# Second experts of a fused transformer block: the links of a tile's chain two tiles apart, banks by matrix, gates on ScalarE

## The reference

```python
scores = softmax(xf @ Wg.T)
expert_weights, expert_indices = top_k(scores, 2)        # of 8 experts
expert_weights = expert_weights / expert_weights.sum(-1, keepdims=True)
h1 = lora_in(xf, W1, b1, A1, B1)                         # 128 -> 256, per expert
h3 = lora_in(xf, W3, b3, A3, B3)
g = silu(h1) * h3
y_e = lora_out(g, W2, b2, A2, B2)                        # 256 -> 128
y = einsum('te,ted->td', gates, y_e)
```

## Time and profile before

| what | value |
|---|---|
| median of three timed runs | 960.75 us (959.2 to 961.38) |
| profiled execution, from its first to its last instruction | 1025.8 us |
| its time outside this span | not given by the trace |
| TensorE, VectorE, GpSimd, ScalarE busy in it | 741.2, 685.5, 575.1, 456.1 us |
| second experts, first turn to last scatter | 851.33 to 995.89 us |
| transfers in it, mean rate 900 to 960 us | 188 GB/s |

### The profile page before, as it was taken

How to read it: one execution, slowest core, us unless ns; L and a number is a source line. 1 busy time by engine, 2 the same in 40 slices (tenths; PEclk the granted TensorE clock), 3 DMA queues, 4 the chain that set the end, 5 groups by cost and what they waited for, 6 DMA issues and landing times. The chain is left out here.

```text
span 1025.8 us, 21613 instructions
## 1 busy us (share of the span) xinstructions
PE 741.2 (72%) x6690; PEld 525.1 (51%) x6690; DVE 685.5 (67%) x3220; ACT 456.1 (44%) x1217; POOL 575.1 (56%) x944
## 2 busy tenths in 40 slices
PE   0687889796749999429892279989898756877750
PEld 0344445453736565225561157766666535777650
DVE  6998899887236876761110848977878564777754
ACT  3656665554004554202231747755556214544430
POOL 6788888868355442026663744455655452556550
PEclk9867887867559999768996559988988667999985
DMA  6300114994129785013542300000000016766517
GB/s 130 69 7 9 40 52 87 98 82 59 41 120 288 246 251 161 11 12 67 87 116 74 112 1 4 8 23 21 25 19 24 25 39 200 220 191 203 160 36 246
DMA packets 98690, 93.94 MB, mean 92 GB/s; under 512 B 37497, under 2 KB 82288, under 8 KB 98001
## 3 DMA queue, kind: packets, MB, share of 16 engines
q1 hardware_dynamic: 91126, 78.82, 31.1%
q0 software_dynamic: 6592, 13.58, 5.2%
q10 hardware_dynamic: 858, 0.17, 0.1%
HBM read 47.24 MB, written 43.19 MB: 88 GB/s over the span
## 5 line engine op out<-in xcount | busy, mean ns | idle before, releaser
L2342 POOL DMA_INDIRECT expert_pairs<-e_ys,e_home x78 | 78.9, 1011 | 76.5 <-DVE e_ys L2364 58.1
L1766 POOL DMA_INDIRECT expert_slots<-r_rows,r_slotu x64 | 63.2, 988 | 47.8 <-DVE r_rows L2095 31.7
L1750 POOL TENSOR_SCALAR a_kb<-a_kr,a_m,a_bk 128x128 f32<-128x128 f32 x128 | 57.5, 449 | 49.5 <-ACT a_kr L1963 32.9
L918 DVE MATCH_REPLACE8 work<-m,work 128x64 f32<-128x64 f32 x384 | 75.6, 205 | 0.0
L2309 PE MATMUL e_ps<-e_XH,e_wh 128*128 128x256 f32 x156 | 49.1, 315 | 26.7 <-DVE e_hh L2376 23.4
L1948 ACT ACTIVATE a_pp<-a_dd 128x512 f32<-128x512 f32 x64 | 40.2, 629 | 59.7 <-DVE a_dd L2135 57.2
L1537 POOL DMA_INDIRECT ex_rows<-rows,slot_source x32 | 30.7, 961 | 53.3 <-POOLq L1215 43.9
L905 DVE MAX8 m<-work 128x8 f32<-128x64 f32 x384 | 56.9, 207 | 0.0
L793 PE MATMUL psf<-filmw,us 97*128 97x512 f32 x64 | 51.3, 897 | 1.1 <-ACT FO L814 1.0
L2174 DVE RECIPROCAL a_rt<-a_pso 128x128 f32<-128x128 f32 x31 | 29.5, 953 | 30.7 <-PE a_pso L1876 21.3
L1591 ACT ACTIVATE ex_hs<-ex_psh,vec 128x512 f32<-128x512 f32 x32 | 20.9, 687 | 65.4 <-remote 36.2
(11 more groups left out here) (443 smaller groups left out, 2388.1 us busy)
## 6 DMA issues: line engine op xcount, KB each, us to landing
expert_slots<-rt_unfilled SPq DMA_DIRECT2D x151, 130.0 KB, 2.9
e_wf<-folded_weights SPq DMA_DIRECT2D x39, 386.0 KB
e_xr<-expert_slots SPq DMA_DIRECT2D x39, 130.0 KB
planes<-rt_zeros SPq DMA_DIRECT2D x4, 1024.0 KB
ew<-in_L_ffn_ew SPq DMA_DIRECT2D x16, 256.0 KB
comb_y<-planes SPq DMA_DIRECT2D x16, 256.0 KB, 5.7
pair_y<-expert_pairs SPq DMA_DIRECT2D x16, 256.0 KB, 5.8
folded_weights<-fold_done SPq DMA_DIRECT2D x8, 384.0 KB, 4.1
```

The source lines that it names most:

```text
L918: return own.did(dve.match_replace(wk_[x.j][:, h, :], m8[x.j][:, h, r, :], src[:, h, :], TAKEN))
L1750: m = pool.tensor_scalar(kb[a.j][:, :, h, :], k, m4[:, h:h + 1], bk4[:, h:h + 1], ALU.mult, ALU.add)
L1766: pool.indirect_dma_start(G.slots, bass.IndirectOffsetOnAxis(ap=slot[:, b, k, t:t + 1], axis=0), rb[b % NB][:, k, t, :], None).then_inc(se ...
L2342: pool.indirect_dma_start(G.pair, bass.IndirectOffsetOnAxis(ap=home[i % NY][:, k:k + 1], axis=0), ys[i % NY][:, k, :], None).then_inc(kept ...
```

## The change

Turn and split go two tiles ahead instead of one (`AHEAD`), with three buffers of the four split operands (`SPLIT`); the second product and what follows it go two tiles behind instead of one (`BEHIND`), with three buffers of `e1_hh`. The banks of the first layer are one for each matrix instead of one for each matrix and half, and there are two sets of them; a first layer waits for the SiLU and the gate operation of the tile two before. SiLU waits for all six matmuls of h1, the gate operation for all of h3. The product by the gate moves from VectorE to ScalarE (`weigh_rows`), and VectorE keeps the places (`places`), for which GpSimd now waits on a semaphore of their own (`named`). The weights get ten buffers instead of eight.

The core of the diff:

```diff
@@ -2240,24 +2240,22 @@
...
-    NX, NW, NY = 12, 8, 6
+    NX, NW, NY = 12, 10, 6
+    AHEAD, BEHIND, SPLIT = 2, 2, 3
...
-        wh, wl = some(2, "wh", [D, 2, NC, P], F32R), some(2, "wl", [D, 2, NC, P], F32R)
...
-        sg, hh = some(2, "sg", [P, NC, STILE]), some(2, "hh", [P, NC, STILE])
+        wh, wl = some(SPLIT, "wh", [D, 2, NC, P], F32R), some(SPLIT, "wl", [D, 2, NC, P], F32R)
...
+        sg, hh = some(2, "sg", [P, NC, STILE]), some(BEHIND + 1, "hh", [P, NC, STILE])
...
-        psh = [[C.ps(f"e1_ps{m}{c}", [P, STILE], ctx) for c in range(NC)] for m in (1, 3)]
+        psh = [[C.ps(f"e1_ps{m}{j}", [P, NC, STILE], ctx) for j in range(2)] for m in (1, 3)]
...
+        s = {n: C.sem("e1_" + n) for n in ("y", "y_sb", "turned", "x_high", "x_low", "w_high", "w_low", "away", "named", "silu", "hh", "h1_ps", "h3_ps")}
...
-                    after(sp, hh_sb[NC - 1], i - NW + 1)
...
             @block.tensor
@@ -2289,29 +2287,35 @@
                 def product(i):
                     j = i % 2
                     after(pe, s["y_sb"], i - 1)
+                    pe.wait_ge(s["hh"], i + 1)
...
-                        pe.wait_ge(hh_sb[c], i + 1)
...
-                            mm = pe.matmul(psy[j][:, k, :], hh[j][:, c, k * P:(k + 1) * P], wf[i % NW][:, 2 * HE + c * D:2 * HE + (c + 1) * D],
+                            mm = pe.matmul(psy[j][:, k, :], hh[i % (BEHIND + 1)][:, c, k * P:(k + 1) * P], wf[i % NW][:, 2 * HE + c * D:2 * HE + (c + 1) * D],
...
                     mm.then_inc(s["y"], 1)
 
...
+                def first(i):
+                    j = i % SPLIT
                     pe.wait_ge(s["x_low"], i + 1)
                     pe.wait_ge(s["w_low"], i + 1)
-                    for c in range(NC):
-                        for m in range(2):
-                            after(pe, hh_sb[c], i)
...
-                            pe.matmul(psh[m][c][:], wl[j][:, m, c, :], XH[j][:], start=False, stop=True).then_inc(h_ps[m][c], 1)
-                    if i > 0:
-                        product(i - 1)
-                product(NTILE - 1)
+                    after(pe, s["silu"], i - 1)
+                    after(pe, s["hh"], i - 1)
+                    for m in range(2):
+                        for c in range(NC):
+                            pe.matmul(psh[m][i % 2][:, c, :], wh[j][:, m, c, :], XH[j][:], start=True, stop=False)
+                            pe.matmul(psh[m][i % 2][:, c, :], wh[j][:, m, c, :], XL[j][:], start=False, stop=False)
+                            mm = pe.matmul(psh[m][i % 2][:, c, :], wl[j][:, m, c, :], XH[j][:], start=False, stop=True)
+                        mm.then_inc(s["h1_ps"] if m == 0 else s["h3_ps"], 1)
+
+                for i in range(AHEAD):
+                    turn(i)
+                for i in range(NTILE + BEHIND):
+                    if i + AHEAD < NTILE:
+                        turn(i + AHEAD)
+                    if i < NTILE:
+                        first(i)
+                    if i >= BEHIND:
+                        product(i - BEHIND)
...
+                    act.activation(wh[i % SPLIT][:], w13(i), ACT.Copy).then_inc(s["w_high"], 1)
...
-                for i in range(NTILE):
-                    if i + 1 < NTILE:
-                        high(i + 1)
...
+                    act.activation(XH[i % SPLIT][:], pst[i % 2][:], ACT.Copy).then_inc(s["x_high"], 1)
+
+                def weigh_rows(i):
+                    act.wait_ge(s["y"], i + 1)
+                    after(act, kept[i % NY], i // NY * S * 16)
+                    for k in range(S):
+                        m = act.activation(ys[i % NY][:, k, :], psy[i % 2][:, k, :], ACT.Copy, scale=xr[i % NX][:, k, D + 1:D + 2])
+                    m.then_inc(s["y_sb"], 1)
+
+                for i in range(AHEAD):
+                    high(i)
+                for i in range(NTILE + BEHIND):
+                    if i + AHEAD < NTILE:
+                        high(i + AHEAD)
+                    if i < NTILE:
+                        act.wait_ge(s["h1_ps"], i + 1)
+                        after(act, s["hh"], i - 1)
+                        for c in range(NC):
+                            k = 2 * HE + NC * D + c
+                            m = act.activation(sg[i % 2][:, c, :], psh[0][i % 2][:, c, :], ACT.Silu, bias=wf[i % NW][:, k:k + 1])
+                        m.then_inc(s["silu"], 1)
+                    if i >= BEHIND:
+                        weigh_rows(i - BEHIND)
...
+                    pool.wait_ge(s["named"], i + 1)
                     pool.wait_ge(s["y_sb"], i + 1)
...
+                    after(dve, s["h3_ps"], i - SPLIT + 1)
+                    dve.tensor_tensor(wl[i % SPLIT][:], w13(i), wh[i % SPLIT][:].bitcast(F32), ALU.subtract).then_inc(s["w_low"], 1)
...
-
-                def take(i):
-                    dve.wait_ge(s["y"], i + 1)
+                    dve.tensor_tensor(XL[i % SPLIT][:], pst[i % 2][:], XH[i % SPLIT][:].bitcast(F32), ALU.subtract).then_inc(s["x_low"], 1)
+
+                def places(i):
                     after(dve, kept[i % NY], i // NY * S * 16)
+                    dve.wait_ge(rows[i % NX], (i // NX + 1) * 16)
...
-                    dve.tensor_tensor(home[i % NY][:], named, away[i % 2][:], ALU.add)
-                    for k in range(S):
-                        m = dve.tensor_scalar(ys[i % NY][:, k, :], psy[i % 2][:, k, :], xr[i % NX][:, k, D + 1:D + 2], None, ALU.mult)
-                    m.then_inc(s["y_sb"], 1)
-
-                low(0)
+                    dve.tensor_tensor(home[i % NY][:], named, away[i % 2][:], ALU.add).then_inc(s["named"], 1)
+
+                for i in range(AHEAD):
+                    low(i)
...
+                    if i + AHEAD < NTILE:
+                        low(i + AHEAD)
...
-                    if i > 0:
-                        take(i - 1)
-                take(NTILE - 1)
+                        dve.wait_ge(s["h3_ps"], i + 1)
+                        dve.wait_ge(s["silu"], i + 1)
+                        after(dve, s["y"], i - BEHIND)
+                        m = dve.scalar_tensor_tensor(hh[i % (BEHIND + 1)][:, c, :], psh[1][i % 2][:, c, :], wf[i % NW][:, k:k + 1], sg[i % 2][:, c, :],
+                                                     ALU.add, ALU.mult)
+                    m.then_inc(s["hh"], 1)
+                    places(i)
...
```

More of the change, by code:

```diff
@@ L2249, in second_experts @@
         xr, wf, ys = some(NX, "xr", [P, S, ROW]), some(NW, "wf", [P, WF]), some(NY, "ys", [P, S, D])
-        wh, wl = some(2, "wh", [D, 2, NC, P], F32R), some(2, "wl", [D, 2, NC, P], F32R)
-        XH, XL = some(2, "XH", [D, STILE], F32R), some(2, "XL", [D, STILE], F32R)
-        sg, hh = some(2, "sg", [P, NC, STILE]), some(2, "hh", [P, NC, STILE])
+        wh, wl = some(SPLIT, "wh", [D, 2, NC, P], F32R), some(SPLIT, "wl", [D, 2, NC, P], F32R)
+        XH, XL = some(SPLIT, "XH", [D, STILE], F32R), some(SPLIT, "XL", [D, STILE], F32R)
+        sg, hh = some(2, "sg", [P, NC, STILE]), some(BEHIND + 1, "hh", [P, NC, STILE])
         away, home = some(2, "away", [P, S]), some(NY, "home", [P, S], U32)
-        psh = [[C.ps(f"e1_ps{m}{c}", [P, STILE], ctx) for c in range(NC)] for m in (1, 3)]
+        psh = [[C.ps(f"e1_ps{m}{j}", [P, NC, STILE], ctx) for j in range(2)] for m in (1, 3)]
         psy = [C.ps(f"e1_psy{j}", [P, S, D], ctx) for j in range(2)]
         pst = [C.ps(f"e1_pst{j}", [P, STILE], ctx) for j in range(2)]
-        s = {n: C.sem("e1_" + n) for n in ("y", "y_sb", "turned", "x_high", "x_low", "w_high", "w_low", "away")}
-        h_ps = [[C.sem(f"e1_h{m}_ps{c}") for c in range(NC)] for m in (1, 3)]
-        silu = [C.sem(f"e1_silu{c}") for c in range(NC)]
-        hh_sb = [C.sem(f"e1_hh{c}") for c in range(NC)]
+        s = {n: C.sem("e1_" + n) for n in ("y", "y_sb", "turned", "x_high", "x_low", "w_high", "w_low", "away", "named", "silu", "hh", "h1_ps", "h3_ps")}
         rows, weights, kept = ([C.sem(f"e1_{n}{j}") for j in range(k)] for n, k in (("rows", NX), ("weights", NW), ("kept", NY)))
@@ L2276, in _ @@
                     after(sp, s["y"], i - NW + 1)
-                    after(sp, hh_sb[NC - 1], i - NW + 1)
+                    after(sp, s["hh"], i - NW + 1)
                     sp.dma_start(wf[i % NW][:], G.folded[bass.ds(e, 1), :, :].rearrange("a p w -> p (a w)")).then_inc(weights[i % NW], 16)
@@ L2296, in product @@
                                            start=(c == 0 and k == 0), stop=(c == NC - 1), skip_group_check=True)
                     mm.then_inc(s["y"], 1)
-                turn(0)
-                for i in range(NTILE):
-                    j = i % 2
-                    if i + 1 < NTILE:
-                        turn(i + 1)
+                def first(i):
+                    j = i % SPLIT
                     pe.wait_ge(s["x_low"], i + 1)
                     pe.wait_ge(s["w_low"], i + 1)
-                    for c in range(NC):
-                        for m in range(2):
-                            after(pe, hh_sb[c], i)
```

(21 more changed lines are left out.)

10 lines of the change are left out of this document (removed).

## The result

The changed kernel takes 974.02 us (median of 8 runs, 964.72 to 985.13), the kernel before 961.21 us beside it (8 runs, 959.2 to 964.1): 1.0092 times as long, 95% interval 1.0049 to 1.0136. The ratio leaves out the three longest runs of the changed kernel, which fell in a slower state of the chip, so it is smaller than that of the two medians, which lie 12.8 us apart. The forecast of 962.2 us was too low and its range ended at 965.

The account below looks back on a forecast made before the run. Three engines were taken as full at once in the second experts, TensorE slowest at 2.54 us a tile. From the 960.75 us median, plus 1.9 for the later start, less 0.5 for the gates: 962.2 us, range 954 to 965.

Parts of the forecast that it names:

- (a): Turn and split two tiles ahead: free in the steady part, tile 0's first layer 1.5 us late, 1.2 us net.
- (b): Second product two tiles behind: first scatter 2.8 us later; end 1.2 to 2.8 us later, taken at 1.9.
- gapless gait: Second experts' stage: TensorE takes tiles without idle time, 2.54 us each; the timed kernel was taken to run so already.
- holds: Waits of about 2 us on TensorE's signals, 34.2 us in the second experts, put down to the profile's recording.
- the first rival: Slower: GpSimd's serial scatters decide the stage's end, at 2.5 to 2.8 us, 963.4 us or up to 965; chance 0.28.
- (c): First-layer banks by matrix in two sets, later SiLU start: nothing gained or lost.
- (e): Ten weight buffers and GpSimd's wait for names: nothing.
- (d): Gates moved from VectorE to ScalarE: 0 to 3.8 us back, taken at 0.5 us.
- The second rival: Faster by a little: timed kernel not gapless, 0.1 to 0.2 us saved a tile, 955 to 959 us; chance 0.17.
- The third: Faster by much: holds are the chip's own, two tiles' distance outlasts them, 34.2 us go, 928 us; chance 0.13.

Follow-up runs that it names:

- before_2: Unchanged copy of the kernel before, on a chip of the 961 us kind: 1.0057 times before, stage 111.7 us.
- ramp1: Changed kernel with the second product one tile behind and, in the start, the third tile's turn after tile 0's first layer: 1.0125 times before, stage 115.1 us.
- both1: Changed kernel with both distances back at one tile; split buffers, banks by matrix and ScalarE's gates kept: 1.0054 times before, stage 112.9 us.
- after_2: Unchanged copy of the changed kernel, on a chip of the 961 us kind: 1.0068 times before, stage 116.8 us.
- dve_rows: Changed kernel with the weighting by gates given back to VectorE: 1.0047 times before, stage 118.0 us.
- warm_before: Kernel before with 22 spare transposes on TensorE at the start of the second experts: 1.0018 times before, stage 111.4 us.
- again_before: Unchanged copy of the kernel before, on a chip of the longer kind: 1038.27 us, 0.9991 times before.
- warm_after: Changed kernel with 28 spare transposes on TensorE at the start of the second experts: 1.0156 times before, stage 117.6 us.
- half_scatter: Changed kernel with one scatter a tile instead of two, pair table filled ahead of the stage: 1.0184 times before, stage 111.5 us.

## Why the prediction was wrong

**The step that failed.** The sum took the later first scatter at 1.9 us, the middle between 1.2 and 2.8. The first scatter came 4.9 us later and the stage ended 5.3 us later. The mechanism of (a) and (b) was right; their sizes were too small, the middle was the wrong choice between them, and 0.5 us ahead of the first scatter stood in the sum at nothing. The 4.9 us by the traces (changed kernel against before_2): 2.35 us up to the first layer, 2.40 from there to the first product, 0.33 less from the product to the result, 0.52 more from the result to the first scatter. Another 0.33 comes during the scatters. Even a forecast with the full 5.3 us would give 966 us, beyond the range, whose upper end went by 2.8.

**The premise.** That the timed kernel was already in the gapless gait of 2.54 us was right: the copy of before shows it, 2.54 us a tile. The reason given was wrong, so this was luck. A profiled execution on the other kind of chip has no holds, so they don't belong to the recording; the 65 us between profile and timed runs are the difference of the two kinds. That 34.2 and 36.2 us nearly made up the 65 was chance. Between before and before_2 the spans differ by 60.0 us, of which 34.9 lie in the second experts. In the first experts the 36.2 us of waiting were mostly no loss: from the first `ex_hs` to the start of the last one 73.5 us passed on the one kind and 64.6 on the other, 8.9 us less. Some 16 us lie elsewhere. It did no harm to the sum: the first layer starts 5.8 us after the first load of rows on either kind.

**Term (a), turn and split two ahead: 1.2 us forecast.** The mechanism was right, the size not. The first layer of tile 0 comes 2.35 us later (8.12 against 5.77), not 1.5. The forecast gave tile 2's rows the landing of tile 1's, 2.24 us; they took 2.97 (829.76 to 832.73), with weights and rows of three tiles asked for by then. Nothing of it came back. ramp1 against both1 puts the distance ahead at 2.1 us of stage, with the third turn moved as well.

**Term (b), product two behind: first scatter 1.2 + 1.64 = 2.8 us later, taken at 1.9.** From the first layer to the first product 7.22 us passed instead of 4.82. These 2.4 us stood as 1.64: the price of a tile at full speed, for a place where TensorE works at the lower clock. The ten more matmuls ahead of the clock's rise, an estimated 0.9 us, would cover the difference. In the copy after_2, with four more and 0.4 us, the stretch was 2.04 us longer, so the estimate fits both; no run takes the low clock away alone. ramp1 to the changed kernel shows 1.7 to 1.9 us for this distance, again with the third turn moved. And the middle of the bounds was no choice between them: in every kernel of the table with all its scatters the last one ended 98.8 to 99.6 us after the start of the first, as the first rival has it.

**Terms (c) and (e), banks, signals, wait for names: nothing forecast.** both1 keeps them and costs 1.2 us. Its first product is 0.65 us later, though it waits for no gate: 20 matmuls ran ahead of the clock's rise against 16, an estimated 0.4 us, and the third turn stood until its rows were there. The result comes to the scatter 0.5 us later, as said above, and the 78 scatters take 99.2 us against 98.8. Which edit makes which of these was not tried.

**Term (d), gates by ScalarE: -0.5 forecast.** dve_rows measured -1.0 to -1.3. The two operations took 364 ns each, below the 0.39 to 0.45 us that were expected. Per tile of the steady part ScalarE was busy 2.11 us, where 2.43 was forecast, and VectorE 2.08, where the prediction has "about 1.95" (2.48 less two operations of 343 ns would be 1.79).

**The sum.** Forecast +1.4; by the stages both1's 1.2 (with (d)'s part in it), 2.1 on the way to ramp1 and 1.9 on to the changed kernel make 5.3, or 0.55% of 961 (5.0 by the copy). Of the rivals the first was right in its place and mechanism, GpSimd's chain, and in its threshold (a pair of scatters takes 2.53 us, over 2.48). Its price of 2.5 to 2.8 us was half of what it is, because it took its first scatter from (a) and (b). The second rival fell, since the old kernel has no gap: a steady 2.54. The third fell as well: no 34 us were to be had on either kind of chip (2.4 us less stage on the longer one).

**What the profile was to show.** TensorE's tile never under 2.54: right in the steady part; two tiles at the end, without a turn, take 2.32. First layer 1 to 2 us later: 2.35. First scatter 2.5 to 3 us later: 4.9. Last scatter more than 3 us, near 5, after the last product is read: 6.6 (934.43 to 940.99). Held matmul pace kept, some 127 in 20 us: wrong for this trace (172); on the other kind of chip 124 to 142.

**What stays open.** The measured 0.92% has an interval of 0.49 to 1.36%, the second measurement gave 0.68% (0.11 to 1.26%). The stage's 0.55% lies in both. The part ahead of the stage is the same program in all of these kernels, yet the first load of rows came anywhere from 818.15 us (warm_before) to 831.04 (after_2), so single executions differ by 13 us there. Whether the rest, 3.5 us or 0.4%, is anything but this spread, which gave a copy 0.57%, cannot be told from these runs.

## What to carry over

When the steady part of a pipeline is a tie of full engines, more distance between its links buys nothing there. Its price is a later first result, and a serial last engine without slack (2.53 of 2.545 us here) carries that to the end, behind results that then come in a bunch. Cost the start with the start's own rows, its clock and the landing times of the first transfers, not with steady ones. And before the gap between a profile and the timed runs is given to the recording, profile a copy of the same kernel beside timed runs on the same chip and look at both numbers together. Two waits that add up to the gap prove nothing; the idle time of the same line without the gap does.

## What the runs showed of the chip

- One program took 963 and 965 us on two chips and 1039 us on a third. On the slower one ScalarE's copy of a turn waited some 2 us, without a cause that the kernel orders, 13 times in a stage (again_before, 24.4 us on `e_XH`, 2.3 at most), with 0.63 of the transfer time in use (862 to 990 us); on a faster one there was no such wait, with 0.81 in use (before_2, 840 to 930 us).
- TensorE's clock was full when it began a wait of 2.37 us shortly after the start of the stage, and at 1.2 GHz behind it (warm_after); around a wait of 1.21 us at the same place it stayed full (warm_before).
- 128 rows of 128 fp32 scattered by GpSimd stand 1.264 us apart when nothing is waited for, 0.96 busy and 0.30 of gap. With a wait ahead of each they were busy 1.27 us on average instead of 0.96 (half_scatter).
